# A padding tensor in front and the turned keys behind: every float32r tensor of a cross-attention and feed-forward kernel begins at a multiple of 2048 bytes of its partition

## The reference, cut to what matters

```
q = layernorm(x) @ Wq + bq;  k = ctx @ Wk + bk;  v = ctx @ Wv + bv      16 heads of 32
a = softmax(clip(q k^T / sqrt(32), -1e4, 1e4));   x = x + (a v) @ Wo + bo
P = layernorm(x) @ U1;  H = gelu(P @ V1 + b1)                           rank 128, width 2048
x = x + (H @ U2) @ V2 + b2
```

## Time and profile before

| | us |
|---|---|
| median of three runs | 563.78 |
| the profiled execution's own time | 563.44 |
| its span, from the first to the last instruction | 561.6 |
| TensorE busy in the span | 551.6 (98%) |
| VectorE busy | 474.0 (84%) |
| GpSimd busy | 376.5 (67%) |
| ScalarE busy | 308.8 (55%) |

### The profile page before, as it was taken

One profiled execution on the slowest core, in us unless ns is written; L12 is line 12 of the kernel. 1 busy time (PEld: TensorE's weight loads), 2 busy tenths in 40 slices (PEclk: granted clock), 3 DMA queues, 4 the chain that ended last, 5 costly groups with the idle time before them and its releaser, 6 DMA issues.

```text
span 561.6 us, 12010 instructions
## 1 busy us (share of the span) xinstructions
PE 551.6 (98%) x4804; PEld 462.2 (82%) x4804; DVE 474.0 (84%) x693; ACT 308.8 (55%) x516; POOL 376.5 (67%) x296
## 2 busy tenths in 40 slices
PE   8999999999999999999999999999999999999996
PEld 7788889888988898889877677888888888888885
DVE  4789999889988998889799567979798897978584
ACT  3465454445444544454455546757575757666663
POOL 2688776788778877886679356747484756565581
PEclk9999999999999999999999999999999999999999
DMA  8522353221333133333412130031211222101012
GB/s 312 174 81 77 109 212 113 96 71 64 112 95 99 42 108 96 104 126 129 132 63 89 58 112 2 19 107 44 68 76 65 74 76 75 58 19 57 19 57 94
DMA packets 25263, 50.36 MB, mean 90 GB/s; under 512 B 2936, under 2 KB 3064, under 8 KB 24824
## 3 DMA queue, kind: packets, MB, share of 16 engines
q1 hardware_dynamic: 24920, 49.07, 25.6%
q10 hardware_dynamic: 288, 0.52, 0.3%
HBM read 32.49 MB, written 16.78 MB: 88 GB/s over the span
## 4 chain that ended last, share of the span: by engine, by line
PE 89%; DVE 7%; DMA 1%; ACT 1%; issue 1%; POOL 0%; SPq 0%; DVEq 0%
PE bank L1018 53%; PE ps_s L1018 15%; PE bank L1096 6%; PE ps_s L1070 6%; PE bank L1112 5%; PE bank L1039 2%; PE bank L1143 2%; DVE once L840 1%; DMA fw<-in_Wk 1%; DVE smax L803 1%; DVE wqo_r L845 1%; DVE ss L794 1%; DVE ssum L808 1%; DVE hs_r L863 1%; PE ps_s L1176 1%
## 5 line engine op out<-in xcount | busy, mean ns | idle before, releaser
L502 POOL TENSOR_TENSOR hs_r<-ss,hs_r 128x512 fp32r<-128x512 f32 x63 | 90.8, 1441 | 91.6 <-ACT hs_r L715 91.0
L628 ACT ACTIVATE ss<-ps_s,once 128x512 f32<-128x512 f32 x128 | 88.1, 689 | 66.8 <-PE ps_s L1018 62.7
L1018 PE MATMUL ps_s<-p1t_r,v_r 128*128 128x512 f32 x384 | 112.2, 401 | 0.0
L1018 PE MATMUL bank<-hs_r,u_r 128*128 128x512 f32 x381 | 108.3, 393 | 0.0
L1018 PE MATMUL bank<-zt_r,wqo_r 128*128 128x256 f32 x768 | 98.7, 284 | 0.4 <-DVE zt_r L756 0.4
L408 POOL TENSOR_TENSOR ss<-ss,smax 128x1232 f32<-128x1232 f32 x32 | 74.8, 2338 | 35.4 <-DVE smax L803 35.4
L1018 PE MATMUL bank<-wqo_r,ot_r 128*128 128x512 f32 x384 | 97.4, 403 | 0.0
L1018 PEld LDWEIGHTS bank<-zt_r,wqo_r 128*128 128x128 f32 x768 | 92.5, 188 | 2.3 <-DVE zt_r L756 0.8
L1018 PEld LDWEIGHTS bank<-hs_r,u_r 128*128 128x128 f32 x381 | 71.5, 188 | 16.7 <-DVE hs_r L863 0.2
L1018 PEld LDWEIGHTS bank<-wqo_r,ot_r 128*128 128x128 f32 x384 | 69.9, 189 | 15.0 <-DVE ot_r L816 0.2
L1018 PEld LDWEIGHTS ps_s<-p1t_r,v_r 128*128 128x128 f32 x384 | 69.8, 188 | 14.4 <-issue 0.4
(11 more groups left out here) (94 smaller groups left out, 821.7 us busy)
## 6 DMA issues: line engine op xcount, KB each, us to landing
xs<-in_x SPq DMA_DIRECT2D x64, 256.0 KB, 3.3
y_between<-xs SPq DMA_DIRECT2D x32, 256.0 KB, 2.0
fw<-y_between SPq DMA_DIRECT2D x4, 1024.0 KB, 5.7
xs<-y_between SPq DMA_DIRECT2D x4, 1024.0 KB, 5.6
out<-fw SPq DMA_DIRECT2D x16, 256.0 KB, 2.0
out<-xs SPq DMA_DIRECT2D x16, 256.0 KB, 2.1
ss<-in_wq SPq DMA_DIRECT2D x2, 512.0 KB, 8.0
xs<-in_Wo SPq DMA_DIRECT2D x1, 1024.0 KB, 9.9
```

Of the source, the lines that this page charges most:

```text
L502: pool.tensor_tensor(hs[:, c % 4, 1, :], hg[:, c % 4, :], hs[:, c % 4, 0, :].bitcast(F32), ALU.subtract)\
L628: act.activation(hg[:, c % 4, :], ps_s[:, c % 4, :], ACT.Gelu_apprx_tanh, bias=b1_c[:, c:c + 1]).then_inc(h_gelu, 1)
L1018: mm = pe.matmul(ps, lhs(a), rhs(c), start=first and i == 0, stop=last and i == len(PASSES) - 1)
```

## The change

A tensor `lead` of 480 float32 (1920 bytes for each partition) that nothing reads or writes is placed ahead of all others, and `kt` is given out behind `z`, `pt`, `vrows` and `once`, ahead of `bias_row`.

```diff
+LEAD = 480
...
+        sb("lead", [P, LEAD])
         wqo_r = sb("wqo_r", [P, 2 * 2 * KD * D], F32R)
         wq_r = wqo_r[:, 0:2 * KD * D].rearrange("p (h k n) -> p h k n", h=2, k=KD)
         wo_r = wqo_r[:, 2 * KD * D:].rearrange("p (h k n) -> p h k n", h=2, k=KD)
         v1_t = sb("v1_r", [P, 2 * FF], F32R)
         v1_r = v1_t[:, :].rearrange("p (h n) -> p h n", h=2)
-        kt_t = sb("kt", [P, G * B * KV])
-        kt = kt_t[:, :].rearrange("p (g b w) -> p g b w", g=G, b=B)
         zt_t = sb("zt_r", [P, 2 * KD * TA], F32R)
...
         y_of = lambda j, b: y_ring[(2 * j + b) % 4]
+        kt_t = sb("kt", [P, G * B * KV])
+        kt = kt_t[:, :].rearrange("p (g b w) -> p g b w", g=G, b=B)
         bias_row = sb("bias_row", [P, D])
```

## The result

The changed kernel takes 567.51 us (median of six runs, 566.68 to 567.71), against 563.59 us for the kernel before beside it (562.42 to 564.05): 3.9 us more, ratio 1.007, 95% interval 1.0061 to 1.008. I had forecast 563.7 us and no difference. The range (558.5 to 566.5) does not hold the time.

The account below looks back on a forecast made before the run. TensorE's number of instructions times their pitch was taken to bound the kernel. All terms were 0 but 0.1 us off at the start: 563.44 less 0.1 is 563.3, with 0.34 for the median 563.7 us; range 558.5 to 566.5.

Parts of the forecast that it names:

- The list of three ways in which the time could move: Whole kernel: matmul pitch, the duration of another engine's instruction that TensorE comes to wait for, or transfers at the start.
- The excess: Float32r matmuls: 8 to 10% over their columns' time, about 19 ns at 512, 10.8 at 256; at most 33.4 us off.
- follows its place in time, not its address: Float32r matmuls: a product's length does not depend on its address modulo 2048, so the pitch changes by 0.
- The other engines: VectorE, GpSimd, ScalarE: moved homes change durations by 0; up to 4% longer instructions would be hidden beside TensorE.
- The keys and the start: Moved `kt` in the scores: 0, bound 1 us either way; first loads: 0.1 us off, bound 0.7 either way.
- A: Float32r matmuls: the homes cause the slow stream, most excess goes, 25 us off, 538 us; chance 0.11.
- B: Float32r matmuls: mixing phases 128 and 544 costs; unmixed, 6.9 us off, 557 us, or 560 with half; chance 0.14.
- C: Float32r matmuls: equal phases of stationary and moving operands collide, 8.1 us more, 572 us, or 566; chance 0.10.
- D: Placement: the first tensor isn't at 128, so homes are off; the forecast's time, next to no chance, within its 0.60.
- The 0.05 for an unhidden layout effect on VectorE or GpSimd: VectorE or GpSimd: a layout effect not hidden beside TensorE, 565 to 568 us; chance 0.05.

Follow-up runs that it names:

- e10: The changed kernel with three small memsets on GpSimd ahead of its subtraction of chunk 1 in each feed-forward block: 561.13 us, ratio 0.996.
- e13: The kernel before, homes untouched, with a 16-element reciprocal on VectorE ahead of its subtraction of chunk 0 from the second feed-forward block on: 568.93 us, ratio 1.0103.
- e1: The changed kernel with GpSimd waiting in chunk 1 of each feed-forward block until VectorE has finished its subtraction of chunk 0: 562.22 us, ratio 0.9982.
- e3: The changed kernel without `lead`, so only `kt` is moved and all float32r homes lie at 128: 567.58 us, ratio 1.0073.
- e4: The kernel before with `lead` alone, `kt` where it was: 563.32 us, ratio 1.0001.
- e6: The changed kernel with a tensor of 32 bytes between `v1_r` and `zt_r`: 562.44 us, ratio 0.9987.
- e9: The kernel before with three one-element memsets on VectorE ahead of its subtraction of chunk 0, from the second feed-forward block on: 563.47 us, ratio 0.9997.
- e11: The kernel before with one 192-element memset on VectorE ahead of its subtraction of chunk 0, from the second feed-forward block on: 563.39 us, ratio 1.0003.
- e5: The kernel before with VectorE waiting, from the second feed-forward block on, ahead of chunk 0's subtraction until GpSimd has ended chunk 1's: 583.62 us, ratio 1.0366.

## Why the prediction was wrong

- **What bounds the kernel.** TensorE's pitch, as read. The list of three ways in which the time could move was right too, and two of them happened; I priced both at 0. The excess was misread: "a slower stream, not only a fixed gap". Where the changed kernel's pitch has settled, it is 120.0 ns at 256 columns and 226.7 at 512, the same 13.3 ns above the columns. (From 227 to 237 ns against 213.3 is 6 to 11%, not 8 to 10, and `kt` has 8 slices of 308 bytes in a partition, not 512; nothing hangs on either.)
- **The pitch: "follows its place in time, not its address".** This step failed, by the prediction's own sign: the pitch of each of the six families moved by more than 1 ns. It compared slices that are multiples of 512 bytes apart, in a kernel where the two homes are always 0 or 416 apart, and so could say nothing of a difference of another size. The hint that there was, 1.37 us for six of `project_u2` and `project_v2`, both with their operands at one phase, was only half of one: `project_v2` got slower by the change. By the table the change is worth 2.1 x 768 ns = +1.6 us on `project_q`, -3.2 x 384 = -1.2 on `project_out`, -2.9 x 384 and -3.1 x 384 = -2.3 on the feed-forward products, -6.2 x 96 = -0.6 on `project_u1` (233.2 to 227.0) and +3.2 x 96 = +0.3 on `project_v2` (227.8 to 231.0): 2.2 us off in all. The changed kernel without a turned block bears this out: e10 is 2.4 us below the kernel before beside it.
- **The other engines, 0, with "up to 4% longer instructions" hidden.** This term turned the sign. I asked whether an operation's duration depends on its home. No run shows that it does: where nothing blocks them, the two subtractions take 0.69 and 1.29 us in both kernels. GpSimd's additions of the earlier trace rows grew from 1397 and 1393 to 1444 and 1446 ns, alike on both tensors, and one can be seen at 1.74 us behind VectorE's held-up subtraction (at 385.83 us). I didn't ask what a TensorE that is a few ns faster sets off: a race between two engines with a margin of 40 ns, in a kernel where 1.80 us for GpSimd's 1.29 us subtraction could be seen in the trace. Six turned blocks at 0.93 us (e13) to 1.06 (6.4 us between e10 and the changed kernel) are 5.6 to 6.4 us. With 2.2 us off for the pitch that is +3.4 to +4.2; measured, +3.9.
- **The keys and the start, 0 and 0.1 us off.** The scores kept 1.06 us. The start can't be told: at 20 us the changed kernel and e1, with the same homes, are already 0.4 us apart.
- **The rivals.** A is out: e3 and e4 show that a true multiple of 2048 gives nothing, and the rows never came near 213 ns. B was nearest in mechanism: the feed-forward products did go to 227 ns where their pitch is steady. It missed that `project_q` gets slower (B had 2 ns off; it is 2.1 on), that only 2.2 of its 6.9 us come, and that the order turns. C has the sign and the time, and not the cause: its rows of 0.71 and longer are not there, those ahead of the wait are 0.68 or 0.69. Nothing speaks for D; that e3, with no home at a multiple, is the same kernel in time and pitch shows that it would not have mattered. The 0.05 for an unhidden layout effect on VectorE or GpSimd, 565 to 568 us, held the time and named the engines, without a mechanism: that the time fell there is luck more than reading.

## What to carry to other kernels

Where two engines exclude each other, look in the trace for pairs that start within 0.1 us of one another; any edit, a faster one too, can turn their order, so fix it by a wait or a short delay before judging the edit (here the wait left 562.2 us, the delay 561.1). Judge a change of layout by the distance from one matmul to the next in each family and by the turned pairs, separately: here they were 2.2 us off and some 6 on. A comparison of rows excludes only the differences that those rows contain.

## What the runs showed of the hardware that I had not expected

- The pitch of float32r matmuls changes with how far apart the two groups of homes are that stationary and moving operands come from, by some 3%: 116.0 to 119.7 ns at 256 columns, 228.7 to 233.2 at 512. With a difference of 0 or 1024 bytes it settles at an even 120 and 226.7 ns (32 cycles of 2.4 GHz more than the columns); `project_q` is then at its slowest and the feed-forward products at their fastest. A family whose own two operands are never apart moves too (`project_u2`, `project_v2`). That the two readers of TensorE meet in SBUF is a reading; no run shows it.
- Who goes first between VectorE and GpSimd is decided within a few ns: by the starts on record VectorE goes first down to 2 ns behind (e10) and no longer at 7 behind (e6). These starts are not exact to such a size (in e9 VectorE's subtraction is on record 8 ns before the first memset that the program has ahead of it). But a memset of VectorE in between kept GpSimd out although GpSimd's start is on record 0.17 us before the subtraction's and 0.04 us before the memset's (e11).
- Waits of TensorE for VectorE of up to 1.9 us (0.7 in the changed kernel) were followed by 3.4 us at a granted clock of 1.2 GHz in three of seven blocks (e5).
